# VectorE holds back one expert's weight splits until GpSimd has issued three gathers (mixture-of-experts block, one core)

## What is computed

```python
x_in = einsum('bct,bcd->bdt', x, weights[itok])
top_p, top_i = top_k(softmax(xt @ gate_w), 2)
for k in range(2):                                   # per choice: the token's rank within its expert, dropped past 160
    buf[e, pos] = xt                                 # gather of rows
    h = gelu(einsum('ecd,edf->ecf', buf, w1) + b1)
    y = einsum('ecf,efd->ecd', h, w2) + b2 + gelu(buf @ wd) @ wu
    out += y[e, pos] * top_p[:, k]
sh = gelu(xt @ sw1 + sb1) @ sw2 + sb2 + gelu(xt @ swd) @ swu
return x + out + 0.2 * sh
```

## Time and profile before

| | us |
|---|---|
| median of 3 runs | 185.01 |
| lowest and highest | 183.78, 187.5 |
| profiled execution, its own time | 186.1 |
| profiled execution, span from first to last instruction | 184.2 |

### The profile page before, as it was taken

One profiled execution on the slowest core, in us unless ns is written; L12 is line 12 of the kernel. 1 busy time (PEld: TensorE's weight loads), 2 busy tenths in 40 slices (PEclk: granted clock), 3 DMA queues, 4 the chain that ended last, 5 costly groups with the idle time before them and its releaser, 6 DMA issues.

```text
span 184.2 us, 4117 instructions
## 1 busy us (share of the span) xinstructions
PE 171.7 (93%) x1442; PEld 166.0 (90%) x1442; DVE 146.9 (80%) x329; ACT 140.1 (76%) x315; POOL 100.8 (55%) x112
## 2 busy tenths in 40 slices
PE   6899999999907969999999999999999999999994
PEld 6776789999907969999999999999999999999993
DVE  3499999999923457998978968978988998899721
ACT  3386889038704489899799989989899999898930
POOL 5637268401835816308857866887848647155600
PEclk9999999999996999999999999999999999999999
DMA  5798000199461219369588678787779479778242
GB/s 133 248 311 285 5 2 4 29 316 344 130 238 48 85 35 311 76 221 247 84 289 258 104 270 238 122 270 234 103 281 252 81 272 232 164 273 143 28 85 64
DMA packets 25981, 31.84 MB, mean 173 GB/s; under 512 B 4668, under 2 KB 22488, under 8 KB 25960
## 3 DMA queue, kind: packets, MB, share of 16 engines
q1 hardware_dynamic: 21816, 26.22, 44.6%
q0 software_dynamic: 3904, 5.25, 16.4%
q10 hardware_dynamic: 240, 0.10, 0.2%
HBM read 26.31 MB, written 5.24 MB: 171 GB/s over the span
## 4 chain that ended last, share of the span: by engine, by line
PE 75%; DVE 11%; DMA 5%; POOL 4%; issue 2%; ACT 1%; DVEq 0%; ACTq 0%
PE y_ps L1038 10%; PE y_ps L1040 10%; PE y_ps L1039 10%; PE hid_ps L1038 9%; PE hid_ps L1040 8%; PE hid_ps L1039 8%; DMA slot_in<-slot_rows,slot_src 5%; PE turn_ps L1040 4%; PE turn_ps L1038 3%; PE turn_ps L1039 3%; PE turn_ps L1217 3%; DVE xct_l L762 1%; DVE hid_l L739 1%; DVE at_place L836 1%; DVE key_values L858 1%
## 5 line engine op out<-in xcount | busy, mean ns | idle before, releaser
L493 POOL DMA_INDIRECT out_rows<-y_row,slot_tok x23 | 38.5, 1673 | 26.9 <-DVE y_row L929 11.6
L479 POOL DMA_INDIRECT slot_in<-slot_rows,slot_src x23 | 31.7, 1379 | 23.6 <-DVE slot_src L888 8.0
L1038 PE MATMUL y_ps<-w_h,hid_h 128*128 128x256 f32 (+2 forms) x128 | 36.8, 288 | 0.0
L1039 PE MATMUL y_ps<-w_l,hid_h 128*128 128x256 f32 (+2 forms) x128 | 36.4, 284 | 0.0
L1040 PE MATMUL y_ps<-w_h,hid_l 128*128 128x256 f32 (+2 forms) x128 | 36.3, 284 | 0.0
L739 DVE TENSOR_TENSOR hid_l<-gelu_f,hid_h 128x320 fp32r<-128x320 f32 (+3 forms) x54 | 26.0, 496 | 8.0 <-ACT hid_h L641 7.6
L1038 PE MATMUL hid_ps<-xs_h,w_h 128*128 128x248 f32 (+6 forms) x96 | 27.8, 290 | 1.5 <-ACT hid_h L641 1.5
L1039 PE MATMUL hid_ps<-xs_l,w_h 128*128 128x248 f32 (+6 forms) x96 | 27.3, 284 | 0.0
L1040 PE MATMUL hid_ps<-xs_h,w_l 128*128 128x248 f32 (+6 forms) x96 | 27.3, 284 | 0.0
L716 DVE TENSOR_TENSOR w_l<-w_raw,w_h 128x512 fp32r<-128x512 f32 x40 | 26.7, 702 | 0.0
L709 DVE TENSOR_TENSOR w_l<-w_raw,w_h 128x512 fp32r<-128x512 f32 x40 | 26.4, 705 | 0.3
(11 more groups left out here) (260 smaller groups left out, 472.1 us busy)
## 6 DMA issues: line engine op xcount, KB each, us to landing
w_raw<-in_L_ffn_w SPq DMA_DIRECT2D x16, 1024.0 KB
w_raw<-in_L_ffn_sw SPq DMA_DIRECT2D x3, 1024.0 KB
x_in<-in_x SPq DMA_DIRECT2D x2, 512.0 KB, 3.6
w_raw<-in_L_ffn_sw SPq DMA_DIRECT2D x2, 512.0 KB, 7.6
slot_rows<-token_row SPq DMA_DIRECT2D x8, 128.0 KB, 4.1
wu_raw<-in_L_ffn_wu SPq DMA_DIRECT2D x24, 32.0 KB
out_rows<-base SPq DMA_DIRECT2D x1, 512.0 KB
slot_in<-slot_rows,slot_src POOLq DMA_INDIRECT x23
```

The source lines that it names most:

```text
L479: pool.indirect_dma_start(out=slot_in[par][0:n, s, :], out_offset=None, in_=x_rows, in_offset=bass.IndirectOffsetOnAxis(ap=slot_src[0:n, e ...
L493: pool.indirect_dma_start(out=out, out_offset=bass.IndirectOffsetOnAxis(ap=slot_tok[0:n, e, s:s + 1].bitcast(U32), axis=0), in_=y_row[0:n, ...
L1038: pe.matmul(out_ap, l_h, r_h, start=start, stop=False)
L1039: pe.matmul(out_ap, l_h, r_l, start=False, stop=False)
```

## The change

GpSimd puts an empty instruction with a signal behind the three requests for the first expert's rows, and VectorE waits for that signal before its first weight split of that expert. Nothing else changes.

```diff
@@
+        rows_asked = sem("rows_asked")
...
@@ gpsimd
             gather(0, 0)
+            pool.engine_nop().then_inc(rows_asked, 1)
             pool.wait_ge(slots_in[0], 16 * ST)
             gather(1, 1)
...
@@ vector
+            dve.wait_ge(rows_asked, 1)
             for c in range(CHUNKS):
                 w1_chunk(c, 1, 1)
             w2_chunk(0, 1, 1)
```

## The result

| | before | after |
|---|---|---|
| median, us | 184.75 (4 runs, 183.78 to 187.5) | 178.5 (4 runs, 177.64 to 179.77) |
| profiled execution, its own time | 186.1 | 179.77 |
| profiled execution, span | 184.2 | 177.7 |

The ratio after/before is 0.9684, with an interval of 0.9596 to 0.9772: the change makes the kernel 3.2% faster. The forecast was 179.2, between 176.8 and 182.7. Executions more than 1.5% above the fastest of the same kernel (here 187.5) are left out of this and the later ratios, while the medians hold all.

A forecast was written before the change was run, and what follows sets the result against it. TensorE bounds the kernel, solid from 66.25 us. Landing 5.3 plus clock 1.3 less VectorE 0.3 was put at 6.4 us: 186.1 - 6.4 = 179.7, or 178.6 against the median; middle 179.2, range 176.8 to 182.7.

The forecast's parts named there:

- The third request: GpSimd's third request for expert 0's rows: starts at 48.02, ends at 49.1, no longer lasting 4.08 us.
- The signal and the wait: Empty instruction and signal on GpSimd cost 0.1 us; VectorE is released at 49.2, 1.0 us later than before.
- Rival B: The empty instruction signals while the third request is still being described; VectorE starts as before, 185 us; chance 0.06.
- The landing: Expert 0's rows land 2.04 us after the request, at 51.1, with no load ahead; worth 5.3 us.
- Rival C: Rows still land late, delivery 4.32 us, at 53.4; gain 4.3, 181.8 us; chance 0.04.
- The clock: TensorE, transposes to expert 0's first matmul: full clock makes 3.45 us into 2.1, worth 1.3 us.
- VectorE behind the wait: VectorE's remaining splits, shared row and `xs_l` end at 53.5, 0.3 us after TensorE is ready: the new limit.
- The second gap: TensorE's 1.48 us idle before 66.25, behind ScalarE, unexplained; kept in the sum, with 1.5 us possible extra gain.
- Rival A: VectorE does not hold the third request, which still lasts 4.08 us; gain 3.4, 182.7 us; chance 0.07.
- Rival D: Experts' stage: shifted GpSimd requests meet VectorE's splits, each costing up to 2.1 us; 189.0 us; chance 0.04.
- at 133.13 in the earlier trace: Experts' stage request lasting only 1.46 us though splits ran on; seemingly let in at a seam between two splits.

The follow-up runs named there:

- The repeat: The changed kernel run once more, unchanged: 178.14 us, ratio to before 0.961.
- the signal-alone profile: The changed kernel without VectorE's wait, leaving only GpSimd's empty instruction and its signal: 185.23 us, ratio to before 1.0006.
- the pair of held-back kernels: Changed kernel plus four extra w1 splits ahead of VectorE's wait: both inputs in SBUF 181.11 us, first input in PSUM 179.34 us.

## Why the prediction was right

**The third request: right.** Forecast 1.07 us from its start (48.02 to 49.09), by 0.80 us behind the last hidden split. Measured 1.06, and 0.79 behind the end of the hidden splits (49.65 to 50.44). The figure 0.79 to 0.81 came back in the changed kernel and in four experiments.

**The signal and the wait: right.** Forecast 0.1 from the request's end to VectorE; measured 0.07. Idle time forecast about 0.9, measured 0.86. Rival B is out: the empty instruction signals behind the request, and alone it does nothing (1.0006).

**The landing: right as a mechanism, and mis-sized in the first profile.** The forecast moved it from 56.42 to 51.1, 5.3 us. Profile to profile it moved 3.06: 1.36 because the first request began later, 0.88 because delivery took 2.92 and not 2.04, and the forecast's 51.1 is otherwise met (51.1 + 1.36 + 0.88 = 53.34). In the six other profiles without a load ahead, delivery took 1.86 to 2.06. Rival C as a rule is out; between its 4.32 and the forecast's 2.04 one execution stands with 2.92.

**The clock: right, at 1.12** (forecast 1.3). The transposes to expert 0 take 2.33 us (forecast 2.1), at a granted clock of 1.00, that is 2.4 GHz.

**VectorE behind the wait: right.** Forecast 4.3 from release to the end of `xs_l`, and VectorE as the limit. The repeat shows 4.23 with VectorE as the limit; in the first profile the rows were later, by 0.80 at `xs_l`.

**The second gap: the step that failed.** The forecast kept its 1.48 us of TensorE's idle time in the sum, and expected 124.3 us from expert 0 to the end of the span; the changed kernel shows 122.0. The gap stands in the first profile of before alone: from expert 0's start to the end of the span it is 124.3 us there, and 122.0 to 122.55 in the nine other profiles, those with a low clock around the transposes among them. Three of these nine kernels hold the third request for 4.1 us as before, so it is not the change that removes the gap. It was in one execution of ten, and a term of the sum should not have been made of it or of its absence. What caused it stays open.

**Why the sum came out all the same.** Between the first two profiles it came out by luck: landing and clock gave 3.06 + 1.12 = 4.2 us where 6.4 were forecast, because the rows were late, and the missing second gap and what lies around it gave 2.3. Without these two chances the forecast holds as follows. Request to expert 0 was to shrink by 11.85 - 5.5 = 6.4 us; it shrank by 5.54 in the first profile and 6.44 in the repeat. Against the signal-alone profile, which equals before within 0.01 us in all three parts of the table and has no second gap, the repeat's span is 182.7 - 176.8 = 5.9 shorter, although its first request began 0.96 later. Between the medians of all runs the gain is 6.3 (first comparison) and 7.0 (repeat). The profiled execution of before had the second gap but also a milder fall of the clock than most: its mean granted clock is 0.991, that of most runs of before 0.98. My estimate from these means: half the clock for a share of 2 x (1 - 0.981) of some 183 us is about 7 us at 1.2 GHz, against 3.3 at 0.991. No trace shows an execution with 0.981.

**Rival A fell, and with it an inference of the Trainium skill.** "SBUF — State Buffer", section "Who interferes with whom", reports that `tensor_tensor` did not stall DMAs, and infers that describing a DMA on GpSimd needs the write interface of the port pair that it shares with VectorE, while `tensor_tensor` takes only the read interface. For indirect DMAs the pair of held-back kernels says otherwise: 3.48 us with two SBUF inputs, 1.07 with one. The same section's rule that a VectorE instruction with two SBUF inputs contends with a GpSimd instruction that reads SBUF agrees. That it is the reading of the row numbers that meets the splits fits that rule but is not shown: every request here is indirect.

**Rival D did not come.** In the experts' stage three requests are shut out in the profile after:

```profile
84.59 2.98 POOL L480 DMA_INDIRECT slot_in<-slot_rows,slot_src  x1 [0.30 <-issue]
```

with the like at 97.89 and 112.14 (2.99 each). The first profile of before has two (2.99, at 104.36 and 118.60), but the change is not the cause: with the signal alone, where nothing is shifted, there are three as well (2.98, at 89.14, 102.88 and 117.14), and so in all profiles but the one with the second gap. Nothing is paid for them: TensorE is busy in all of 119.00 us from 56 to 175.

## What to carry to other kernels

If a DMA that GpSimd describes lasts several times as long as its equals, look at what VectorE does beside it: a row of instructions with two SBUF inputs and no pause can hold it, and here it then ended about 0.8 us after the row. A pause in that row was enough, be it a wait or a tiny other instruction. It is worth something only where somebody is waiting for the transfer: the requests held in the experts' stage cost nothing. Follow the release on to its second order: here the held request also let a 1 MB load in ahead of 64 rows, and the idle time took TensorE's clock with it. And take a term of a sum from one profile only if a second execution is likely to show it; measure from the local event (here the request), not from the start of the span.

## What the runs showed of the hardware

**The hold spans several instructions.** Five splits in a row shut a request out for all of 3.1 us, though each of them ends; a 128 x 1 memset between two of them lets it in. I had expected every boundary to have a chance, as at 133.13 in the earlier trace rows. What decides whether a bare boundary lets a request in stays open. Even the second request of the changed kernel ran beside an unbroken row of instructions with two SBUF inputs (47.23 to 49.65) and took only 1.04 us; it ended at 49.08, 0.83 after the end of one of them (`wd_l`, 47.90 to 48.25). So such a row can hold a request and need not.

**It meets GpSimd's arithmetic too.** This is why the first request of the changed kernel was late. GpSimd and VectorE of the changed kernel in the ranking of the experts:

```profile
25.34 4.45 POOL L527 TENSOR_TENSOR tie<-count 128x8 f32<-128x8 f32 x1
29.86 0.27 POOL L528 TENSOR_TENSOR tie<-tie,col_of 128x8 f32<-128x8 f32 x1
```

```profile
25.42 0.68 DVE L718 TENSOR_TENSOR w_l<-w_raw,w_h 128x512 fp32r<-128x512 f32 x1
...
29.04 0.68 DVE L741 TENSOR_TENSOR hid_l<-cond_g,hid_h 128x512 fp32r<-128x512 f32 x1
```

An instruction of 128 x 8, 0.42 to 0.83 us in other profiles (0.83 in the first of before), lasts 4.45, until VectorE's unbroken row of two-input splits is over at 29.72. The chain to the requests hangs on it: further on, VectorE waits for the end of GpSimd's ranking.

```profile
36.83 0.29 DVE L845 TENSOR_TENSOR picked<-chosen,rank_at 128x128 f32<-128x128 bf16 x1 [1.30 <-POOL steps_down L544]
```

In the repeat and in two experiments the first request was as late for another reason: there the transposes of the router's scores, at 16.39 in the first profile of before, came at 17.84 to 17.93.

**Delivery of 2.92 us in that profile.** The same held instruction seems to be behind it. SyncE reads the experts' order, which GpSimd writes at the end of the ranking, before it loads an expert's weights: in this profile GpSimd has written it at 36.14 and SyncE's loads begin at 37.12, in the repeat at 33.32 and 34.28. The first stores of `out_rows` follow these loads (40.58 and 41.29, in the repeat 37.74 and 38.45). Packets of about 1 KB, the size of such a row, then fill SyncE's queue q1 while the rows of expert 0 are asked for. DMA queues in 48 to 50 (packets, MB, share), where GpSimd's queue q0 has no packet at all:

```profile
q1 hardware_dynamic: 762, 0.75, 107.4%
```

and in the repeat, with the requests at the same times:

```profile
q0 software_dynamic: 65, 0.20, 37.8%
q1 hardware_dynamic: 299, 0.06, 14.3%
```

The rows start to move in 50 to 51 in the one and in 48 to 49 in the other. The expert's own small loads do not tell the two apart: SyncE issues them at 48.42 to 50.43 in this profile and at 48.44 to 50.46 in the repeat. That the older traffic made the 0.9 us is argued from these rows; no run isolates it. Seams in the ranking stage, which might take some 1.3 us from the executions in which L527 is held, were not tried.
